# Squares move to the transpose banks, and nine convolution units rotate through six PSUM banks

## What is computed

```
gate, xBC, dt = split(layernorm(x) @ in_proj_w.T)       # 8192 + 10240 + 128 columns
xBC = silu(causal_conv4(xBC) + conv_b)                  # depthwise, 4 taps
x, B, C = split(xBC)                                    # 128 heads of 64; 8 groups of state 128
Y_diag, states, Y_off = chunked state-space scan of x*dt with B, C and exp(cumsum(A*dt))
y = (Y_diag + Y_off + D*x) * silu(gate)
var = mean(y*y over the 1024 columns of a group)
y = y * rsqrt(var + 1e-5) * norm_w
out = y @ out_proj_w.T
```

## Time and profile before

| | |
|---|---|
| timed runs | 2189.47 us median (2186.38 to 2189.52) |
| profiled execution | 2184.44 us, span of its instructions 2182.7 us |
| PE busy | 2009.5 us (92%) |
| DVE, ACT, POOL busy | 65%, 54%, 49% |
| mean granted TensorE clock | 0.968 |

### The profile page before, as it was taken

How to read it: one execution, slowest core, us unless ns; L and a number is a source line. 1 busy time by engine, 2 the same in 40 slices (tenths; PEclk the granted TensorE clock), 3 DMA queues, 4 the chain that set the end, 5 groups by cost and what they waited for, 6 DMA issues and landing times.

```text
span 2182.7 us, 39215 instructions
## 1 busy us (share of the span) xinstructions
PE 2009.5 (92%) x11776; PEld 1659.4 (76%) x11776; DVE 1419.1 (65%) x2710; ACT 1176.9 (54%) x2553; POOL 1065.8 (49%) x955
## 2 busy tenths in 40 slices
PE   3899999999999999999999899999999889989898
PEld 2677888788878887887778788778887768766776
DVE  6696589649864976597569657964886461186314
ACT  2585368437843874386449536853785225422341
POOL 1397149615950693179228813971496025240433
PEclk7899999999999999999999999999999999999999
DMA  2452035214511441233124203520451149932795
GB/s 83 127 151 82 25 112 151 64 31 124 160 51 41 122 144 40 80 113 114 40 85 145 92 25 99 153 75 21 121 154 50 58 137 354 356 84 81 281 400 170
DMA packets 143908, 261.75 MB, mean 120 GB/s; under 512 B 19536, under 2 KB 35920, under 8 KB 143696
## 3 DMA queue, kind: packets, MB, share of 16 engines
q1 hardware_dynamic: 134848, 231.35, 33.7%
q0 software_dynamic: 7520, 24.65, 3.5%
q10 hardware_dynamic: 1328, 3.15, 0.4%
HBM read 233.38 MB, written 25.69 MB: 119 GB/s over the span
## 4 chain that ended last, share of the span: by engine, by line
issue 31%; DVE 28%; PE 24%; POOL 14%; ACT 1%; DMA 1%; DVEq 1%; POOLq 0%; SPq 0%; ACTq 0%
PE bank L1503 14%; DVE Y L1214 7%; POOL Y L716 6%; PE bank L1786 5%; DVE Y L1223 3%; DVE mem L1202 3%; PE bank L1798 3%; DVE mem L1182 2%; DVE E L1245 2%; POOL Y L666 2%; DVE quad L1214 2%; POOL spare L692 2%; DVE Y L1239 2%; POOL mem L692 2%; POOL wl L699 1%
## 5 line engine op out<-in xcount | busy, mean ns | idle before, releaser
L1503 PE MATMUL bank<-xh,wh 128*128 128x512 f32 x1288 | 534.2, 415 | 85.2 <-DVE cv L1254 38.1
L1503 PE MATMUL bank<-xh,wl 128*128 128x512 f32 x1288 | 512.4, 398 | 0.0
L1503 PE MATMUL bank<-xl,wh 128*128 128x512 f32 x1288 | 511.4, 397 | 0.0
L699 POOL TENSOR_TENSOR wl<-raw,wh 128x512 fp32r<-128x512 f32 x144 | 185.2, 1291 | 494.1 <-ACT wh L851 494.1
L1503 PEld LDWEIGHTS bank<-xh,wh 128*128 128x128 f32 x1288 | 248.3, 193 | 144.1 <-DVE cv L1254 41.4
L1214 DVE SCALAR_TENSOR_TENSOR Y<-bank,cpar,Y 128x511 f32<-128x511 f32 (+2 forms) x384 | 287.0, 747 | 28.7 <-ACT Y L896 19.7
L1503 PEld LDWEIGHTS bank<-xh,wl 128*128 128x128 f32 x1288 | 247.5, 192 | 56.1
L1503 PEld LDWEIGHTS bank<-xl,wh 128*128 128x128 f32 x1288 | 248.8, 193 | 46.9 <-issue 0.5
L716 POOL TENSOR_TENSOR Y<-Y,gt 128x512 f32<-128x512 f32 x128 | 176.8, 1381 | 151.2 <-DVE gt L1258 150.2
L1503 PE MATMUL bank<-wh,ah 128*128 128x512 f32 x576 | 230.1, 400 | 18.6 <-DVE al L1430 17.9
L1503 PE MATMUL bank<-wl,ah 128*128 128x512 f32 x576 | 227.6, 395 | 0.0
(11 more groups left out here) (214 smaller groups left out, 3877.6 us busy)
## 6 DMA issues: line engine op xcount, KB each, us to landing
mem<-c_rows SPq DMA_DIRECT2D x128, 256.0 KB, 3.8
mem<-wffn_d SPq DMA_DIRECT2D x62, 512.0 KB
E<-e_rows SPq DMA_DIRECT2D x256, 96.0 KB, 3.5
raw<-wconv_d SPq DMA_DIRECT2D x80, 256.0 KB, 2.8
cv<-c_rows SPq DMA_DIRECT2D x64, 256.0 KB, 4.0
spare<-c_rows SPq DMA_DIRECT2D x64, 256.0 KB, 4.3
raw<-wgate_d SPq DMA_DIRECT2D x64, 256.0 KB, 2.7
raw<-wout_d SPq DMA_DIRECT2D x64, 256.0 KB, 2.7
```

What stands on the lines that cost most here:

```text
L699: inc(pool.tensor_tensor(wl[:, W_SLOT[p], :], raw[:, R_SLOT[p], :], wh[:, W_SLOT[p], :], ALU.subtract), w_lo)
L1503: got = mm(out, l, r, start=first and n == 0, stop=last and n == 2)
```

## The change

The squares from n = 2 on go to banks 3 and 5 in turn. These are the banks of the transposes, whose last user is `xs_ok` of u = 14 and 15, for which the squares of n = 2 and 3 now wait; from n = 4 on a square waits for the add of n - 2. Bank 0 is thus never taken by squares, and gate units rotate through banks 0, 1 and 2 throughout: unit 30 waits for the gate of unit 27 instead of the add of n = 7. Units 0 to 8 use banks 6, 7, 4, 1, 2, 0, 6, 7, 4, and from unit 9 on k - 2 modulo 3 is the bank. Since units 6, 7 and 8 now are the last convolution units in the banks of the scan, the first state product (step 10) waits for `conv_ok` of unit 8 (the ninth) instead of unit 2 (the third). Unit 20 is in bank 0 now, last used by unit 17, and was in bank 1, last used by unit 18. No instruction is added, removed or put at another place on its engine; only banks and what is waited for differ.

```diff
         def sq(n):
-            return bank[SQ_BANK if n < SQ_LATE else (DG, OF)[n % 2]][:, :]
+            return bank[TR[n % 2]][:, :]
...
-        SQ_BANK, SQ_LATE = 0, 8
-        BANKS = [ST, OF, DG] + [(k - 2) % 3 for k in range(3, NCONV)] \
-            + [1 + n % 2 if n < SQ_LATE else (n - SQ_LATE + 1) % 3 for n in range(NGATE)] + [t % 3 for t in range(TT)]
+        EARLY = [ST, OF, DG, 1, 2, 0, ST, OF, DG]
+        BANKS = EARLY + [(k - 2) % 3 for k in range(len(EARLY), NBIG)]
...
             if k < 3:
                 before(eng, (s_ok, off_ok, ydiag_ok)[k], i, UNITS)
-                before(eng, ss_add, i, NGATE - BATCH)
-                return
-            if k == NCONV + SQ_LATE + 2:
-                now(eng, ss_add, i, SQ_LATE - BATCH)
                 return
...
-                        if n == BATCH:
-                            now(act, conv_ok, i, NCONV - 2)
-                        elif BATCH < n < SQ_LATE:
-                            now(act, ss_add, i, n - BATCH)
-                        elif n >= SQ_LATE + 2:
-                            now(act, ss_add, i, n - 2 - BATCH + 1)
-                        elif n == SQ_LATE:
-                            now(act, ydiag_ok, i, UNITS)
-                        elif n == SQ_LATE + 1:
-                            now(act, off_ok, i, UNITS)
+                        if n >= 2 * BATCH:
+                            now(act, ss_add, i, n - 2 * BATCH + 1)
+                        elif n >= BATCH:
+                            now(act, xs_ok, i, UNITS - 2 + n - BATCH + 1)
...
                         if u:
                             now(pe, s_ok, i, u)
                         else:
-                            now(pe, conv_ok, i, 3)
+                            now(pe, conv_ok, i, len(EARLY))
                             now(pe, tr_act, i, 2)
```

## The result

The changed kernel takes 2116.21 us (median of 4 runs, 2115.74 to 2117.52) against 2188.01 us for the kernel before (median of 4, 2186.38 to 2189.52). The ratio is 0.9673 with a 95% interval of 0.9656 to 0.969, so 3.3% faster. The forecast was 2124 us, in a range of 2106 to 2145. The two profiled executions differ by 68.7 us (2184.44 and 2115.74).

The account below looks back on a forecast made before the run. PE's late starts at units 20 and 30 were taken to bound the kernel, with POOL setting the pace between. Terms 38.1 + 18.1 + 5.6 + 3.2 + 0.8 = 65.8 us, off 2189.5, gave 2123.7 us; range 2106 to 2145.

Parts of the forecast that it names:

- Unit 30: PE at unit 30: the wait for DVE's add goes (38.1 us) and the clock stays up (18.1 us).
- Unit 20 and the early units: Units 20 and 0 to 8: earlier starts, mostly given back to POOL, gain 5.6 + 3.2 + 0.8 us.
- rival A: Gate stretch, units 27 to 36: something still holds it at 3.10 us per unit; 27 us lost, 2151 us; chance 0.10.
- the ring: Steps 28 and 29: DVE, ACT and DVE again wait in turn, adds 3.10 us apart, since one bank holds all squares.
- the wait of unit 20: PE idle 3.05 us before unit 20: removing it gains 5.6 us, plus 3.2 us of clock in two groups.
- B: Units 20 to 27: PE's lead is kept as POOL's stretch shrinks; 19 us more gained, 2105 us; chance 0.07.
- C: Steps 10 and 24 to 26: new PE waits lower the clock once per group; costs 18 us, 2142 us; chance 0.11.
- D: Step 10: PE stops for unit 8, the clock falls and following steps drag; 30 us slower, 2220 us; chance 0.03.

Follow-up runs that it names:

- unit 20 alone: Kernel before with unit 20 moved to bank 0 and the first square there waiting for its gate; unit 30's stall stays: 2175.88 us, ratio 0.9956.
- six early banks alone: Kernel before with nothing changed but early convolution units rotating through six banks: 2185.52 us, ratio 0.9996.
- unit 30 alone: Kernel before with gate units kept to banks 1 and 2 up to unit 31, so unit 30 avoids the squares' bank: 2140.78 us, ratio 0.9792.
- unit 20 waits again: Changed kernel with unit 20 also waiting for the end of unit 18, as before the change: ratio 0.9759.

## Why the prediction was right, and where it was not

**The place and the mechanism hold.** Unit 27 was forecast at 128.9 us behind the group's first unit and stands at 128.79. From unit 27 to 36, 24.6 us were forecast, and it is 24.61. POOL is busy throughout its stretch, which begins 0.48 us earlier in the group (98.87 us behind the first unit, 99.35 before) where some 0.5 were forecast, and PE's new waits were put at 0.8 and 1.4 us for its decays and about 1 us for unit 8; they are 0.80, 1.30 and 1.24.

**Unit 30** (56.2 us): 57.8 measured (254.6 - 196.8). Of the 1.6 us between, 1.3 are my reading: the idle time of a row is counted from the modelled end of the matmul before, so the real lateness is 4.92 us (7.64 between units 29 and 30, less 2.72) and not 4.76.

**Unit 20 and the early units** (9.6 us): 11.1 measured (1042.9 - 1031.9 at unit 27), of which 1.2 are the first group's first units at a higher clock and belong to no term. Unit 6 comes 0.72 us earlier and not 0.48, the first state product 0.2 us later and not 0.4, and DVE's copy behind it gains 0.13 us, where 0.1 was forecast. That PE's three microseconds are given back to POOL is shown twice, by the run with unit 20 alone (26.4 us early, 17.2 given back) and by the one that relieves POOL (18 us more).

**The sum** (65.8 us): 68.7 by the profiled executions, 71.8 by the medians. The 3 us between are no effect of the change: the profiled execution of before lay 3.6 us below the median of its runs, that of after 0.5.

**The reason I gave for rival A was wrong**, though A did not come. I wrote that units 28 to 35 would run at 2.72 us because the second square bank breaks the ring. The run with both waits moved and the squares left in one bank keeps the ring at 3.11 us, and PE does not notice. The gates there have two banks up to unit 31, and the ring's lag of 0.4 us per step brings them within 0.34 us of holding PE up; from unit 32 on they have three again. In the changed kernel the ring is in fact broken: from 601.36 us on the adds of the third group come after 3.11, 1.85 and 3.20 us, 2.72 on average, and unit 30 finds its bank free for 3.8 us (603.36 less the end of the gate of unit 27, 598.83 + 0.69). None of that was needed. The ring mattered only because unit 30 waited for one of its members.

**The terms do not add as I added them.** I priced the wait of unit 20 at 8.8 us, by the clock that it cost in the kernel before. That is right as a part of the way from before to after if it goes first (9.6 us measured alone). But with unit 30 freed first, the same wait costs 27 us by the ratios (0.9792 against 0.967) and 23 by the table, and put back into the changed kernel 19 to 21 us. My sum came out right because the change frees both units: what unit 30 loses in its own stretch (57.8 us) is then gained whole, and the falls behind unit 20, which I had not thought of, have no wait to follow. Why the clock falls behind a wait of 3 us in some groups and not in others stays open. In groups 2 to 8 it fell in 1 of 14 where unit 30 stalled in the group ahead (the kernel before and the one with six early banks alone), and in 13 of 14 where it did not (unit 30 alone, unit 20 waits again); in the first group, which has no stall of unit 30 ahead of it, it fell in all four kernels. But the last group of the kernel before fell in spite of the stalls ahead of it. Freeing unit 30 also shortens the group, and so shifts the moment at which unit 20 comes, and the turns of 8.5 and 7.35 us would fit a cause of that kind. No run parts the stall from the shift.

**Rivals.** B (lead kept) falls with the unit 20 run. C and D needed a clock that falls at the new small waits; the largest is 1.30 us, and the clock stays at 1.00 from 70 to 1660 us. By the Trainium skill (TensorE: Matmul & The Clock Gate, A second HAM failure mode: psum-queue depth-cycling) rotating banks with small idle times would have kept the clock going up and down; this trace does not agree for waits of 1.3 us, and agrees that idle PE time is what brings it down, at 2.9 us sometimes and at 3.5 us always. The other rule of the Trainium skill that I weighed (Perfetto Trace Analysis, Matmuls: rotate through different banks) was worth about 1 us where it was applied broadly (six early banks). The 58 us of the stretch behind unit 27 came from one unit's bank.

## What to carry to other kernels

Count a bank's wait by what it makes wait, not by how many banks are free: two waits out of 44 units were all of this gain, and moving the squares out of the way bought nothing that a gate two units later in the shared bank had not bought. A long idle time of PE costs its length and the slow matmuls behind it, so price both from the rows, and do not expect the gains of freeing two such waits one by one (10 and 45 us here) to add up to that of freeing both (72). When a freed engine comes early and nothing follows, look for the engine that is busy for every microsecond in between; here relieving POOL of four subtractions was worth 18 us, once DVE had a hole to put them in.

## What the runs showed of the hardware

Behind idle times of PE the granted clock fell to the lower of its two levels (1.2 of 2.4 GHz) and came back within one or two units. Behind 4.76 us it fell every time (unit of 2.72 us: 4.18 to 5.29 us), behind 3.52 us every time (4.19 to 5.29), behind 2.7 to 3.05 us in some groups only (step of 5.76 us: 7.13 to 8.63), and behind 1.3 us never in the mixer. Of eight groups it fell in two behind 3.05 us (the kernel before), in eight behind 3.0 (unit 30 alone), in seven behind 2.85 (unit 20 waits again) and in one behind 2.75 (six early banks alone). That the same wait can be free or cost 2.9 us in two kernels that differ only at another place of the group, I had not expected.
